# A prologue's second norm and its first two gated groups, taken batch by batch in 256-column matmuls and banks of their own

## The chip, the core and the metric

One core of a Trainium2 chip. The metric is the device time of one execution in microseconds. The program works on its eight pairs of sequences one after another, in one launch. The kernel before took 775.72 us (median of 3 runs, 775.19 to 776.27).

## What is computed

The input x has 16 sequences of 256 rows and 256 features, and so has the context. One layer of cross attention (an mLSTM form with 8 heads of 32), then a gated feed-forward net with hidden size 1024, both with a norm ahead of them and added to the residual. Cut to what matters:

```python
x = x + xattn(layernorm(x), ctx, ctx, ifgate_w, ifgate_b, outnorm_w)
z2 = layernorm(x)
h = silu(z2 @ w1.T * w1_s) * (z2 @ w2.T * w2_s)
h = gelu(h @ h1.T * h1_s)
h = gelu(h @ h2.T * h2_s)
x = x + h @ w3.T * w3_s
```

## The kernel before, in words

Two sequences (batches 0 and 1) make a pair: 512 rows in Q = 4 tiles of 128, tiles 0 and 1 of batch 0, tiles 2 and 3 of batch 1. The eight pairs run one behind the other. In the steady part the attention of pair i + 1 is woven into the feed-forward net of pair i; the attention of pair 0 stands alone in a prologue, and the change is at its end.

Each engine has its program written out by hand, and semaphores tie them. In the prologue's last part VectorE computes the second norm of pair 0 into `z2`, one tile at a time (`first_norm_apply`, L811), and TensorE transposes each tile into PSUM (`turn_first`, L1263): features on partitions, rows on the free axis. PSUM is two tensors of four banks, `ps_a` and `ps_f`, each bank 512 float32 wide. The features make two halves c of 128; half c of all 512 rows goes to bank c of `ps_a`. Then the transposed norm is split for exactness in two float32r parts: ScalarE copies it to the high part `z2_hi` (`take_z2T`, L668 and L670), VectorE subtracts that from the PSUM value to the low part `z2_lo` (L1053, L1055). In the trace these two are named after the buffers in which they lie, h_hi and h_lo.

The gated layer has KH = 8 groups m of 128 hidden units. A group needs two products, with w1 and with w2, each over two feature halves and two parts: eight matmuls of 512 columns into two banks of `ps_f`, banks 0 and 1 for even m, 2 and 3 for odd m. Group 0 of pair 0 is `first_swiglu` (L1444), which orders the eight by what is ready: high half 0, high half 1, low half 0, low half 1. The other groups are `swiglu` (L1434 for the high part, L1435 for the low part). ScalarE applies silu to the first product (L678), VectorE multiplies with the second (L1067) and signals `s_hf`; ScalarE and VectorE then make the high and low part of the result (L682, L1072). A group m of 2 or more waits for `s_hf` of group m - 2, since it writes the same banks:

```python
if m >= 2:
    pe.wait_ge(s_hf, KH * i + m - 1)
```

Behind the gated layer come two hidden layers of 8 groups with 16 matmuls each (`hidden`, L1468 and L1469) and the projection (L1503, L1504), which has matmuls of 256 columns.

`keep_clock` (L1587) issues matmuls of the identity that nobody reads; it stands twice near the change, with 24 before the transposes and with 2 behind them. `running_max` (L885) and `offsets` (L892 to L894) belong to pair 1's gates and stand on VectorE around the split. SP waits for the running maximum, stores it (`keep_rows`, L351) and spreads it over the partitions (`spread_max`, L362) for the masks of pair 1 (L917). `turn_rows` (L1336) transposes the gate rows behind group 2. ACT names ScalarE, DVE VectorE, PE TensorE and PEld its weight loads.

Of the kernel before, what the change touches and what calls it, by code (L numbers as in the profile page):

```python
# [7 lines left out]
ALU = mybir.AluOpType  # L8
ACT = mybir.ActivationFunctionType
AX = mybir.AxisListType  # L10
F32 = mybir.dt.float32
# [4 lines left out]
P = 128  # L16
BATCH, SEQ, DIM = 16, 256, 256
HEADS, DH = 8, 32
HID = 1024
TILES = SEQ // P  # L20
CH = DIM // P
KH = HID // P
# [10 lines left out]
W = 2  # L33
PAIRS = BATCH // W
NT = W * SEQ
Q = W * TILES
# [37 lines left out]
def build(nc, x, ctx_tok, ctx_t, gate_w, gate_b, outnorm_w, w_cols, scales, w3_s, out):  # L74
    with ExitStack() as stack:
        def sb(name, shape, dt=F32):
            return stack.enter_context(nc.sbuf_tensor(name, shape, dt))

        def sem(name):
            return stack.enter_context(nc.semaphore(name))  # L80
# [8 lines left out]
        z2_hi, z2_lo = h_hi[1][:, 0:CH], h_lo[1][:, 0:CH]  # L89
# [25 lines left out]
        z2 = num[:, 0:Q * DIM].rearrange("p (q d) -> p q d", q=Q)  # L115
# [7 lines left out]
        ident = sb("ident", [P, P])  # L123
# [16 lines left out]
        ps_f = stack.enter_context(nc.psum_tensor("ps_f", [P, 4, NT], F32))  # L140
        ps_a = stack.enter_context(nc.psum_tensor("ps_a", [P, 4, NT], F32))
# [25 lines left out]
        s_z2_first = sem("s_z2_first")  # L167
        s_z2T_first = sem("s_z2T_first")
        s_z2hi_first = sem("s_z2hi_first")
        s_z2lo_first = sem("s_z2lo_first")  # L170
# [51 lines left out]
        s_z2T = sem("s_z2T")  # L222
        s_z2hi = sem("s_z2hi")
        s_z2lo = sem("s_z2lo")

        s_ab = sem("s_ab")
# [16 lines left out]
        def first(j):  # L243
            return isinstance(j, int) and j == 0
# [29 lines left out]
        def score_out(j, b, rowgrp):  # L274

            return ps_f[:, rowgrp] if first(j) and b else ps_a[:, rowgrp]

        def value_out(j, b, t):

            if first(j):  # L280
                return (ps_f if b else ps_a)[:, 2 + t, 0:HEADS * DV]
            return ps_a[:, 2 + b, 0:HEADS * DV]
# [8 lines left out]
        def reuse(eng, semaphore, value):  # L291

            if not (isinstance(value, int) and value <= 0):
                eng.wait_ge(semaphore, value)
# [11 lines left out]
        def weights_in(eng, layer):  # L306
            eng.wait_ge(s_wgt[layer], 16 * sum(n == layer for n, _ in LOADS))
# [246 lines left out]
        def _(act):  # L554
# [109 lines left out]

            def take_z2T(j):
                if first(j):
                    act.wait_ge(s_z2T_first, 1)
                    act.activation(z2_hi[:, 0], ps_a[:, 0], ACT.Copy).then_inc(s_z2hi_first, 1)  # L668
                    act.wait_ge(s_z2T, 1)
                    act.activation(z2_hi[:, 1], ps_a[:, 1], ACT.Copy).then_inc(s_z2hi, 1)  # L670
                    return
                act.wait_ge(s_z2T, j + 1)
                act.activation(z2_hi, ps_a[:, 0:CH], ACT.Copy).then_inc(s_z2hi, 1)
# [96 lines left out]
        def _(dve):  # L770
# [96 lines left out]
            def shift_g(j):  # L867
                n = SCAN_STEPS * j
                f = f_row
                dve.wait_ge(s_scan, n + 1)  # L870

                g = rows[ROW_G:ROW_G + BH]
                dve.scalar_tensor_tensor(g, g, CAP, f, ALU.mult, ALU.add).then_inc(s_scan, 1)
                dve.wait_ge(s_scan, n + 2)
# [5 lines left out]
            def running_max(j):  # L880
                n = SCAN_STEPS * j
                f, m = f_row, m_row
                g = rows[ROW_G:ROW_G + BH]
                reuse(dve, s_mst, 16 * (j - 1))
                dve.tensor_tensor_scan(m, g, g, -MASKED, ALU.max, ALU.max).then_inc(s_scan, 1)  # L885
                dve.wait_ge(s_scan, n + 3)
# [162 lines left out]

            def take_z2T(j):  # L1050
                if first(j):
                    dve.wait_ge(s_z2hi_first, 1)
                    dve.tensor_tensor(z2_lo[:, 0], ps_a[:, 0], z2_hi[:, 0].bitcast(F32), ALU.subtract).then_inc(s_z2lo_first, 1)  # L1053
                    dve.wait_ge(s_z2hi, 1)
                    dve.tensor_tensor(z2_lo[:, 1], ps_a[:, 1], z2_hi[:, 1].bitcast(F32), ALU.subtract).then_inc(s_z2lo, 1)  # L1055
                    return
                dve.wait_ge(s_z2hi, j + 1)
                dve.tensor_tensor(z2_lo, ps_a[:, 0:CH], z2_hi.bitcast(F32), ALU.subtract).then_inc(s_z2lo, 1)
# [161 lines left out]
            scan_f(1)  # L1220
            first_norm_apply(2, xs[0], z2, s_z2_first)
            shift_g(1)
            running_max(1)
            take_z2T(0)
            offsets(1)
            dve.wait_ge(s_scl, 16)
            for i in range(PAIRS):
# [14 lines left out]
        def _(pe):  # L1242
# [15 lines left out]
            def turn_first(src, ready, half_done, done):  # L1258

                for q in range(Q):  # L1260
                    pe.wait_ge(ready, q + 1)
                    for c in range(CH):
                        last = pe.transpose(ps_a[:, c, q * P:(q + 1) * P], src[:, q, c * P:(c + 1) * P], ident[:])  # L1263
                        if q == Q - 1:
                            last.then_inc(done if c else half_done, 1)
# [145 lines left out]
            def columns(u, col, width, as_is):  # L1411

                if as_is:
                    slot = ORDER.index(u) % STAGE
                    return stage[:, slot * UNIT + col:slot * UNIT + col + width]
                return wgt[:, u * UNIT + col:u * UNIT + col + width]
# [4 lines left out]
            def swiglu(i, m, as_is):  # L1421
# [13 lines left out]
                        last = pe.matmul(ps_f[:, bank + half], w, moving(z2_lo[:, c], as_is), start=False, stop=(c == CH - 1))  # L1435
                last.then_inc(s_ab, 1)

            def first_swiglu():

                for part, landed in ((z2_hi, (s_z2hi_first, s_z2hi)), (z2_lo, (s_z2lo_first, s_z2lo))):  # L1440
                    for c in range(CH):
                        pe.wait_ge(landed[c], 1)
                        for half, base in enumerate((UNIT_W1, UNIT_W2)):
                            last = pe.matmul(ps_f[:, half], columns(base, c * P, P, False), part[:, c],  # L1444
                                             start=(part is z2_hi and c == 0), stop=(part is z2_lo and c == CH - 1))
                last.then_inc(s_ab, 1)

            def hidden(i, layer, m, ks, as_is):
                group = KH * layer + m
# [77 lines left out]
            def batch(i, a_stage, g_stage, as_is=False, last=False):  # L1527
                j, g = i + 1, i + 2
                if as_is:
                    pe.wait_ge(s_y, W * i)  # L1530
                weights_in(pe, 0)
                if not first(i):
                    pe.wait_ge(s_z2lo, i + 1)
                if first(i):
                    first_swiglu()
                for m in range(1 if first(i) else 0, KH):
                    swiglu(i, m, as_is)
                    if first(i) and m == 2:
                        turn_rows(1)
                    if a_stage and m == 4:  # L1540
                        scores(j, 0)

                def after_2(m):
                    if a_stage and m == 3:
                        scores(j, 1)
                    if a_stage and m == 5:
                        make_state(j)
                        values(j, 0, 0)
                        values(j, 0, 1)

                def after_3(m):
                    if g_stage and m == 2:
                        gates(g)
                    if a_stage and m == 7:
                        turn_z2(j)
                    if g_stage and m == 7:
                        turn_rows(g)

                def within_2(m):
                    if a_stage and m == 7:  # L1560
                        read_state(j)
                        values(j, 1, 0)
                        values(j, 1, 1)

                def between_2(k):
                    pass

                def between_3(k):
                    if g_stage and k == 3:
                        turn_z(g)  # L1570

                def within_3(m):
                    pass

                weights_in(pe, 1)
                hidden_layer(i, 0, as_is, between_2, within_2, after_2)
                weights_in(pe, 2)
                hidden_layer(i, 1, as_is, between_3, within_3, after_3)
                weights_in(pe, 3)
                project(i, as_is, last)  # L1580
                if last:
                    count_inexact()

            def keep_clock(products, bank=3):

                for _ in range(products):
                    pe.matmul(ps_f[:, bank, 0:P], ident[:], ident[:], start=True, stop=True)  # L1587
# [30 lines left out]
            plain_gates_normed(1)  # L1618
            keep_clock(24, 1)
            pe.wait_ge(s_zTe, 2)  # L1620
            turn_first(z2, s_z2_first, s_z2T_first, s_z2T)
            keep_clock(2, 1)
            for i in range(PAIRS):
                batch(i, i + 1 < PAIRS, i + 2 < PAIRS, last=i == PAIRS - 1)

# [54 lines left out]
```

## Time and profile before

| what | us |
|---|---|
| median of 3 runs | 775.72 (775.19 to 776.27) |
| the profiled execution | 775.79 |
| its span | 773.9 |
| TensorE busy | 764.5 (99%) |
| weight loads busy | 640.6 (83%) |
| VectorE busy | 545.8 (71%) |
| ScalarE busy | 381.6 (49%) |
| GpSimd busy | 50.9 (7%) |
| mean granted TensorE clock | 0.996 |

The span is what the profiler saw between the first and the last instruction; the time of the execution has 1.9 us more around it. An engine counts as busy while one of its instructions runs; matmuls are pipelined, and their ends are modelled, so that the step from one start to the next tells more than the duration. The granted clock is the share of full speed (2.4 GHz) that TensorE got.

### The profile page before, as it was taken

What the parts mean: (1) busy time and instruction counts of PE and PEld (TensorE: products, weight loads), DVE (VectorE), ACT (ScalarE), POOL (GpSimd) and SP (SyncE); (2) the same over time, 40 slices, a digit from 0 to 9 for tenths busy, and PEclk for the clock granted to TensorE, in tenths of its full rate; (3) what the DMA queues carried; (4) which work ended last, traced back from release to release, by engine and by line L of the source; (5) the groups of instructions that cost most, each with busy time, mean ns of one, the idle gap of its engine ahead of it and who ended that gap; (6) DMA issues with size and microseconds to landing.
All of it is one profiled execution on the core that took longest, in us unless ns stands there. A gap on an engine that the chain in (4) does not pass through costs nothing.

```text
span 773.9 us, 14930 instructions
## 1 busy us (share of the span) xinstructions
PE 764.5 (99%) x6170; PEld 640.6 (83%) x6170; DVE 545.8 (71%) x1294; ACT 381.6 (49%) x570; POOL 50.9 (7%) x63
## 2 busy tenths in 40 slices
PE   8999999999999999999999999999999999999997
PEld 7878888878888888878888888888889788888886
DVE  6787867586856969578675877758695684965544
ACT  3455645464554733556445564636435562445331
POOL 3300020000200011000200002000020000000000
PEclk9999999999999999999999999999999999999999
DMA  8933010501122000320005000130102100541540
GB/s 338 368 124 115 29 30 28 191 1 35 52 100 92 28 30 27 122 71 29 30 28 189 2 30 29 69 151 9 50 29 110 54 1 3 185 142 29 162 137 29
DMA packets 14615, 63.43 MB, mean 82 GB/s; under 512 B 2016, under 2 KB 2896, under 8 KB 11728
## 3 DMA queue, kind: packets, MB, share of 16 engines
q1 hardware_dynamic: 12960, 50.12, 18.7%
q0 software_dynamic: 1296, 11.53, 3.8%
q8 instruction: 49, 0.80, 0.4%
q10 hardware_dynamic: 288, 0.79, 0.3%
q14 instruction: 22, 0.18, 0.1%
HBM read 53.94 MB, written 8.50 MB: 81 GB/s over the span
## 4 chain that ended last, share of the span: by engine, by line
PE 85%; DVE 11%; ACT 2%; issue 1%; POOL 0%; POOLq 0%; DVEq 0%; ACTq 0%
PE ps_f L1468 24%; PE ps_f L1469 23%; DVE decay L917 8%; PE ps_f L1434 8%; PE ps_f L1435 7%; PE ps_f L1503 4%; PE ps_f L1504 4%; PE ps_a L1356 2%; PE ps_a L1379 2%; DVE decay L933 2%; PE ps_a L1246 2%; PE ps_f L1587 1%; PE ps_a L1282 1%; PE ps_f L1302 1%; PE ps_a L1407 1%
## 5 line engine op out<-in xcount | busy, mean ns | idle before, releaser
L1468 PE MATMUL ps_f<-h_hi,wgt 128*128 128x512 f32 x1024 | 401.7, 392 | 0.0
L1469 PE MATMUL ps_f<-h_lo,wgt 128*128 128x512 f32 x1024 | 398.8, 389 | 0.0
L1468 PEld LDWEIGHTS ps_f<-h_hi,wgt 128*128 128x128 f32 x1024 | 192.2, 188 | 41.6 <-issue 0.6
L1469 PEld LDWEIGHTS ps_f<-h_lo,wgt 128*128 128x128 f32 x1024 | 192.3, 188 | 38.8
L691 ACT ACTIVATE work<-ps_f,scl 128x512 f32<-128x512 f32 x128 | 87.5, 684 | 161.2 <-PE ps_f L1469 160.6
L1076 DVE TENSOR_TENSOR h_lo<-work,h_hi 128x512 fp32r<-128x512 f32 x128 | 86.5, 689 | 98.2 <-ACT h_hi L696 97.1
L1434 PE MATMUL ps_f<-h_hi,wgt 128*128 128x512 f32 x252 | 99.8, 396 | 0.0
L1435 PE MATMUL ps_f<-h_lo,wgt 128*128 128x512 f32 x252 | 98.7, 392 | 0.0
L678 ACT ACTIVATE work<-ps_f,scl 128x512 f32<-128x512 f32 x64 | 44.1, 689 | 98.2 <-PE ps_f L1435 96.3
L696 ACT ACTIVATE h_hi<-work 128x512 fp32r<-128x512 f32 x128 | 81.0, 633 | 4.1
L1067 DVE SCALAR_TENSOR_TENSOR work<-ps_f,scl,work 128x512 f32<-128x512 f32 x64 | 48.0, 750 | 47.0 <-ACT work L678 47.0
L917 DVE SCALAR_TENSOR_TENSOR decay<-decay,cols,future 128x128 f32<-128x128 f32 x224 | 64.5, 362 | 0.0
L1503 PE MATMUL ps_f<-wgt,h_hi 128*128 128x256 f32 x256 | 62.3, 285 | 0.0
L1504 PE MATMUL ps_f<-wgt,h_lo 128*128 128x256 f32 x256 | 61.7, 283 | 0.0
L1434 PEld LDWEIGHTS ps_f<-h_hi,wgt 128*128 128x128 f32 x252 | 47.3, 188 | 14.7 <-DVE work L1067 3.8
L1435 PEld LDWEIGHTS ps_f<-h_lo,wgt 128*128 128x128 f32 x252 | 47.4, 188 | 8.6
L1504 PEld LDWEIGHTS ps_f<-wgt,h_lo 128*128 128x128 f32 x256 | 49.1, 192 | 0.0
L1503 PEld LDWEIGHTS ps_f<-wgt,h_hi 128*128 128x128 f32 x256 | 49.0, 192 | 0.0
L621 ACT ACTIVATE decay<-decay 128x1024 f32<-128x1024 f32 x28 | 29.7, 1061 | 35.3 <-DVE decay L917 35.3
L1072 DVE TENSOR_TENSOR h_lo<-work,h_hi 128x512 fp32r<-128x512 f32 x64 | 43.7, 682 | 0.8
L682 ACT ACTIVATE h_hi<-work 128x512 fp32r<-128x512 f32 x64 | 39.9, 623 | 2.4 <-DVE work L1067 2.4
L933 DVE SCALAR_TENSOR_TENSOR decay<-ps_a,decay 128x512 f32<-128x512 f32 x60 | 37.1, 677 | 0.7 <-PE ps_a L1356 0.7
(195 smaller groups left out, 701.1 us busy)
## 6 DMA issues: line engine op xcount, KB each, us to landing
decay<-m_rows SPq DMA_DIRECT2D x14, 1024.0 KB, 6.1
decay<-w_cols SPq DMA_DIRECT2D x22, 512.0 KB, 4.2
wgt<-w_cols POOLq DMA_DIRECT2D x5, 1024.0 KB, 11.8
v_aug<-ctx_tok SPq DMA_DIRECT2D x8, 528.0 KB, 4.0
wgt<-w_cols POOLq DMA_DIRECT2D x2, 2048.0 KB, 14.4
x_kept<-xs SPq DMA_DIRECT2D x8, 512.0 KB, 2.6
xs<-x SPq DMA_DIRECT2D x7, 512.0 KB, 3.6
ctxT<-ctx_t SPq DMA_DIRECT2D x7, 512.0 KB, 3.3
```

The source lines that it names most:

```text
L691: act.activation(work[:, m % GELU], ps_f[:, (turn_of(i) + m) % 4], ACT.Gelu, scale=scl[:, 2 + layer, m:m + 1]).then_inc(s_gelu, 1)
L696: act.activation(h_hi[1 - layer][:, m], work[:, m % GELU], ACT.Copy).then_inc(s_hi, 1)
L917: last = dve.scalar_tensor_tensor(part, part, cols[:, t, row:row + 1], future[:], ALU.subtract, ALU.add)
L933: dve.scalar_tensor_tensor(s, score_out(j, b, r).rearrange("p (c n) -> p c n", c=CH), SCORE_SCALE, s, ALU.mult, ALU.mult)\
L1067: dve.scalar_tensor_tensor(work[:, 2 + m % 2], ps_f[:, bank], scl[:, 1, m:m + 1], work[:, m % 2], ALU.mult, ALU.mult).then_inc(s_hf, 1)
L1076: dve.tensor_tensor(h_lo[1 - layer][:, m], work[:, m % GELU], h_hi[1 - layer][:, m].bitcast(F32), ALU.subtract).then_inc(s_lo, 1)
L1434: pe.matmul(ps_f[:, bank + half], w, moving(z2_hi[:, c], as_is), start=(c == 0), stop=False)
L1435: last = pe.matmul(ps_f[:, bank + half], w, moving(z2_lo[:, c], as_is), start=False, stop=(c == CH - 1))
L1468: pe.matmul(ps_f[:, bank], w, moving(h_hi[layer][:, k], as_is), start=(k == 0), stop=False)
L1469: last = pe.matmul(ps_f[:, bank], w, moving(h_lo[layer][:, k], as_is), start=False, stop=(k == KH - 1))
L1503: pe.matmul(to, moving(h_hi[0][:, k, q * P:(q + 1) * P], as_is), w, start=(k == 0), stop=False)
L1504: last = pe.matmul(to, moving(h_lo[0][:, k, q * P:(q + 1) * P], as_is), w, start=False, stop=(k == KH - 1))
```

## The change

The transposed norm of batch b goes to banks 2b and 2b + 1 of `ps_a`, into the first 256 columns of each, one bank per feature half. ScalarE's copy and VectorE's subtraction take a batch at a time, both halves in one instruction of 128 x 2 x 256. `first_turn_z2` takes the place of `turn_first` for z2, and the two `keep_clock` products behind it are gone. `first_swiglu` now holds groups 0 and 1, in matmuls of 256 columns: for batch 0 the high parts of group 0 and group 1, then the low parts of both; for batch 1 high and low of group 0, then high and low of group 1. The list `steps` writes this order out. VectorE does its split before the running maximum of pair 1.

```diff
+        def first_z2T(b):
+            return ps_a[:, W * b:W * b + CH, 0:SEQ]
...
             def take_z2T(j):
                 if first(j):
-                    act.wait_ge(s_z2T_first, 1)
-                    act.activation(z2_hi[:, 0], ps_a[:, 0], ACT.Copy).then_inc(s_z2hi_first, 1)
-                    act.wait_ge(s_z2T, 1)
-                    act.activation(z2_hi[:, 1], ps_a[:, 1], ACT.Copy).then_inc(s_z2hi, 1)
+                    for b, (turned, done) in enumerate(((s_z2T_first, s_z2hi_first), (s_z2T, s_z2hi))):
+                        act.wait_ge(turned, 1)
+                        act.activation(z2_hi[:, :, b * SEQ:(b + 1) * SEQ], first_z2T(b), ACT.Copy).then_inc(done, 1)
                     return
...
                 if first(j):
-                    dve.wait_ge(s_z2hi_first, 1)
-                    dve.tensor_tensor(z2_lo[:, 0], ps_a[:, 0], z2_hi[:, 0].bitcast(F32), ALU.subtract).then_inc(s_z2lo_first, 1)
-                    dve.wait_ge(s_z2hi, 1)
-                    dve.tensor_tensor(z2_lo[:, 1], ps_a[:, 1], z2_hi[:, 1].bitcast(F32), ALU.subtract).then_inc(s_z2lo, 1)
+                    for b, (high, done) in enumerate(((s_z2hi_first, s_z2lo_first), (s_z2hi, s_z2lo))):
+                        at = slice(b * SEQ, (b + 1) * SEQ)
+                        dve.wait_ge(high, 1)
+                        dve.tensor_tensor(z2_lo[:, :, at], first_z2T(b), z2_hi[:, :, at].bitcast(F32), ALU.subtract).then_inc(done, 1)
                     return
...
             shift_g(1)
+            take_z2T(0)
             running_max(1)
-            take_z2T(0)
             offsets(1)
...
+            def first_turn_z2():
+
+                for q in range(Q):
+                    b, t = q // TILES, q % TILES
+                    pe.wait_ge(s_z2_first, q + 1)
+                    for c in range(CH):
+                        last = pe.transpose(first_z2T(b)[:, c, t * P:(t + 1) * P], z2[:, q, c * P:(c + 1) * P], ident[:])
+                    if t == TILES - 1:
+                        last.then_inc(s_z2T if b else s_z2T_first, 1)
+
             def first_swiglu():
 
-                for part, landed in ((z2_hi, (s_z2hi_first, s_z2hi)), (z2_lo, (s_z2lo_first, s_z2lo))):
+                high, low = (z2_hi, (s_z2hi_first, s_z2hi)), (z2_lo, (s_z2lo_first, s_z2lo))
+                steps = [(0, m, part) for part in (high, low) for m in range(2)] + [(1, m, part) for m in range(2) for part in (high, low)]
+                for b, m, (part, landed) in steps:
+                    at = slice(b * SEQ, (b + 1) * SEQ)
+                    pe.wait_ge(landed[b], 1)
                     for c in range(CH):
-                        pe.wait_ge(landed[c], 1)
                         for half, base in enumerate((UNIT_W1, UNIT_W2)):
-                            last = pe.matmul(ps_f[:, half], columns(base, c * P, P, False), part[:, c],
+                            last = pe.matmul(ps_f[:, 2 * m + half, at], columns(base, (m * CH + c) * P, P, False), part[:, c, at],
                                              start=(part is z2_hi and c == 0), stop=(part is z2_lo and c == CH - 1))
-                last.then_inc(s_ab, 1)
+                    if b == W - 1 and part is z2_lo:
+                        last.then_inc(s_ab, 1)
...
-                for m in range(1 if first(i) else 0, KH):
+                for m in range(2 if first(i) else 0, KH):
...
-            turn_first(z2, s_z2_first, s_z2T_first, s_z2T)
-            keep_clock(2, 1)
+            first_turn_z2()
```

TensorE's order at the end of the prologue, before the change: the transposes (of z2, which lies in num), the two clock products, group 0 (L1444), and the first rows of group 1.

```order
L1587 MATMUL ps_f<-ident 128x128 x24
L1263 MATMUL ps_a<-ident,num 128x128 x8
L1587 MATMUL ps_f<-ident 128x128 x2
L1444 MATMUL ps_f<-h_hi,wgt 128x512 x4
L1444 MATMUL ps_f<-h_lo,wgt 128x512 x4
L1434 MATMUL ps_f<-h_hi,wgt 128x512
L1435 MATMUL ps_f<-h_lo,wgt 128x512
```

The same place in the changed kernel, where L1459 is the matmul of the new `first_swiglu`; the last two rows are the first of group 2.

```order
L1603 MATMUL ps_f<-ident 128x128 x24
L1446 MATMUL ps_a<-ident,num 128x128 x8
L1459 MATMUL ps_f<-h_hi,wgt 128x256 x8
L1459 MATMUL ps_f<-h_lo,wgt 128x256 x8
L1459 MATMUL ps_f<-h_hi,wgt 128x256 x4
L1459 MATMUL ps_f<-h_lo,wgt 128x256 x4
L1459 MATMUL ps_f<-h_hi,wgt 128x256 x4
L1459 MATMUL ps_f<-h_lo,wgt 128x256 x4
L1436 MATMUL ps_f<-h_hi,wgt 128x512
L1437 MATMUL ps_f<-h_lo,wgt 128x512
```

Group 0 was the first eight matmuls of 512 columns. Now its share of the thirty-two is spread: four of the first eight, four of the second eight, and the next eight; the last of it is the 24th, and the last eight are group 1's.

VectorE's order at the same place, before: the last norm step, the shift, the running maximum, the two splits, the three rows of the offsets, the product of group 0.

```order
L811 TENSOR_SCALAR num<-xs,mv,nw 128x256 x4
L873 SCALAR_TENSOR_TENSOR rows<-rows,state 16x256
L885 SCALAR_TENSOR_TENSOR state<-rows 16x256
L1053 TENSOR_TENSOR h_lo<-ps_a,h_hi 128x512
L1055 TENSOR_TENSOR h_lo<-ps_a,h_hi 128x512
L892 TENSOR_TENSOR rows<-state 16x256
L893 TENSOR_SCALAR rows<-rows,state 16x128
L894 TENSOR_SCALAR rows<-state 16x128
L1067 SCALAR_TENSOR_TENSOR work<-ps_f,scl,work 128x512 x2
```

And in the changed kernel:

```order
L813 TENSOR_SCALAR num<-xs,mv,nw 128x256 x4
L875 SCALAR_TENSOR_TENSOR rows<-rows,state 16x256
L1057 TENSOR_TENSOR h_lo<-ps_a,h_hi 128x2x256 x2
L887 SCALAR_TENSOR_TENSOR state<-rows 16x256
L894 TENSOR_TENSOR rows<-state 16x256
L895 TENSOR_SCALAR rows<-rows,state 16x128
L896 TENSOR_SCALAR rows<-state 16x128
L1069 SCALAR_TENSOR_TENSOR work<-ps_f,scl,work 128x512 x2
```

The running maximum (L885, now L887) has gone behind the two splits; the rest keeps its order. SP's list of transfers is the same in both.

## Rows read from the trace of the kernel before

**Rows 1.** The page, part 1: busy time, share of the span, instructions.
```profile
PE 764.5 (99%) x6170; PEld 640.6 (83%) x6170; DVE 545.8 (71%) x1294; ACT 381.6 (49%) x570; POOL 50.9 (7%) x63
```

**Rows 2.** The page's chain by engine; who waited for whom (us, times, longest).
```profile
PE 85%; DVE 11%; ACT 2%; issue 1%; POOL 0%; POOLq 0%; DVEq 0%; ACTq 0%
...
PEld ps_f L1434 <- DVE work L1067: 3.8, 21, 0.3
```

**Rows 3.** Timeline, TensorE, 48 to 56 us: start, us, engine, instruction, [idle before <- releaser].
```profile
49.33 1.31 PE L1263 MATMUL ps_a<-ident,num 128*128 128x128 f32 x8
50.48 0.61 PE L1587 MATMUL ps_f<-ident 128*128 128x128 f32 x4
51.32 1.16 PE L1444 MATMUL ps_f<-h_hi,wgt 128*128 128x512 f32 x4 [0.22 <-ACT h_hi L668]
52.31 1.12 PE L1444 MATMUL ps_f<-h_lo,wgt 128*128 128x512 f32 x4
53.27 0.39 PE L1434 MATMUL ps_f<-h_hi,wgt 128*128 128x512 f32 x1
...
54.86 0.39 PE L1435 MATMUL ps_f<-h_lo,wgt 128*128 128x512 f32 x1
55.14 0.50 PE L1434 MATMUL ps_f<-h_hi,wgt 128*128 128x512 f32 x1
```

**Rows 4.** Timeline, TensorE, 49.6 to 49.75 us: the first four transposes.
```profile
49.33 0.67 PE L1263 MATMUL ps_a<-ident,num 128*128 128x128 f32 x4
```

**Rows 5.** Timeline, ScalarE, 50 to 57 us.
```profile
50.58 0.60 ACT L668 ACTIVATE h_hi<-ps_a 128x512 fp32r<-128x512 f32 x1 [1.12 <-PE ps_a L1263]
...
53.53 0.69 ACT L678 ACTIVATE work<-ps_f,scl 128x512 f32<-128x512 f32 x1 [1.87 <-PE ps_f L1444]
```

**Rows 6.** Timeline, VectorE, 50 to 57 us.
```profile
50.19 0.42 DVE L873 SCALAR_TENSOR_TENSOR rows<-rows,state 16x256 f32<-16x256 f32 x1
50.64 0.68 DVE L885 TENSOR_TENSOR_SCAN state<-rows 16x256 f32<-16x256 f32 x1
51.35 0.69 DVE L1053 TENSOR_TENSOR h_lo<-ps_a,h_hi 128x512 fp32r<-128x512 f32 x1
51.96 0.68 DVE L1055 TENSOR_TENSOR h_lo<-ps_a,h_hi 128x512 fp32r<-128x512 f32 x1
...
53.32 0.27 DVE L894 TENSOR_SCALAR rows<-state 16x128 f32<-16x128 f32 x1
54.33 0.75 DVE L1067 SCALAR_TENSOR_TENSOR work<-ps_f,scl,work 128x512 f32<-128x512 f32 x1 [0.74 <-ACT work L678]
```

**Rows 7.** Timeline, TensorE and its weight loads in a projection: matmuls of 256 columns.
```profile
135.89 0.28 PE L1504 MATMUL ps_f<-wgt,h_lo 128*128 128x256 f32 x1
136.01 0.28 PE L1503 MATMUL ps_f<-wgt,h_hi 128*128 128x256 f32 x1
...
135.89 0.19 PEld L1503 LDWEIGHTS ps_f<-wgt,h_hi 128*128 128x128 f32 x1
```

**Rows 8.** Groups by form, ScalarE, 0 to 140 us: count, busy us, mean ns.
```profile
L656 ACT ACTIVATE num<-ps_a 128x528 f32<-128x528 f32 x1 | 0.6, 612 | 0.2 <-PE ps_a L1379 0.2
```

**Rows 9.** Windows: us, busy of PE, PEld, DVE, ACT, POOL; PEclk, DMA share, GB/s.
```profile
34.00:37.40 3.40, 3.40 (x33) 3.40 (x33) 2.52 (x4) 0.00 (x0) 0.00 (x0) 1.00 1.03 424
37.40:40.80 3.40, 3.40 (x14) 2.39 (x14) 2.44 (x8) 2.37 (x5) 0.00 (x0) 0.51 0.86 345
...
48.00:55.00 7.00, 6.70 (x40) 5.17 (x38) 5.99 (x16) 3.21 (x5) 0.00 (x0) 1.00 0.20 55
```

**Rows 10.** Timeline, SP and VectorE; of the decay tile, transfers from issue to landing.
```profile
51.35 0.33 SPq L351 DMA_DIRECT2D m_rows<-state  x1
52.78 0.80 SPq L362 DMA_DIRECT2D decay<-m_rows  x2
...
70.70 9.21 DVE L917 SCALAR_TENSOR_TENSOR decay<-decay,cols,future 128x128 f32<-128x128 f32 x32
...
DMA to landing us min/median/max: 4.8/5.9/7.1
```

## Prediction

> **What bounds the kernel now.** I read the page first: TensorE is busy 99% of the 773.9 us span [rows 1], and the chain that ended last is 85% TensorE [rows 2]. So what sets the end is the stream of matmuls, and in the list of waits the entry that bears on the place of the change is small: the weight loads of the gated layer waited for VectorE's gating step 21 times, 3.8 us in all, 0.3 us at the most [rows 2]. A change at one place of the prologue can then move the end by what it moves the stream behind that place, and by nothing more. The profiled execution took 775.79 us; its span lacks 1.9 us of that, and it lies 0.07 us above the median of the three runs, 775.72. A measurement can tell some 0.2%, 1.55 us, from no change.
>
> The place is 48 to 56 us. There I read the timelines of TensorE, ScalarE and VectorE beside each other. The norm's four tiles are transposed from 49.33 to 50.64 [rows 3]; ScalarE begins to copy channel half 0 at 50.58 [rows 5], and the first gated matmul starts at 51.32, 0.14 us after that copy has ended at 51.18 [rows 3, 5]. Group 0 needs eight 512-column matmuls: four from 51.32, four from 52.31, the last ending at 53.43 [rows 3], and silu starts 0.10 us later, at 53.53 [rows 5]. Silu 0.69 us, VectorE's gating product from 54.33 to 55.08 [rows 6]: then banks 0 and 1 may be written again, and group 2, which writes them, starts at 55.14 [rows 3]. From silu's start to group 2's start it is 1.61 us. Meanwhile group 1 runs from 53.27, its eighth matmul starting at 54.86; 7 steps in 1.59 us make 0.227 us each, so it would leave TensorE free at 55.09 [rows 3]. This is what the reader is to see: in the kernel before, the work of group 1 just covers silu and product of group 0. Two chains, one on TensorE and one over ScalarE and VectorE, end within 0.05 us of each other, and everything of batch 0 and later queues behind group 2.
>
> **The change, term by term.**
> *First start.* Batch 0 of the norm is tiles 0 and 1. Their four transposes end at 50.00 [rows 4]. The copy can start about 0.08 us later (between silu's 0.10 and the smaller gap at the old copy), at 50.08. It reads 512 elements per partition as before, out of two banks now. A two-bank read of 528 elements took 612 ns, against 0.60 us for 512 out of one [rows 5, 8], so I charge nothing for the second bank. It ends at 50.68; plus 0.14 us, the first gated matmul starts at 50.82, **0.50 us earlier**. The two clock products (four matmul records from 50.48 [rows 3]) go; they lay in a wait, and cost or give nothing.
>
> *Splitting low.* VectorE is free at 50.61, after the shift [rows 6], and the running maximum no longer stands ahead. It takes batch 0's low part from 50.80 to 51.49 and batch 1's until about 52.12 (0.69 and 0.68 us, overlapping as in the rows [rows 6]). TensorE wants them after eight and after twenty matmuls, later than 51.7 and 53.1. No wait there; the waits inside the old group 0 are gone.
>
> *The matmuls.* Sixteen of 512 columns become thirty-two of 256. Matmuls of 256 columns in the same types start 0.12 us apart, with their weight loads of 0.19 us overlapping [rows 7]. So the two groups want 32 x 0.12 = 3.84 us, plus some 0.08 for the first after a pause, where sixteen wanted 16 x 0.227 = 3.63. The lower bound of the step is half of 0.227, 0.114; the upper one is the load's own 0.19, if loads did not overlap here. I take 0.12, the row of the same form. The pair of groups ends at about 54.74 instead of 55.09.
>
> *When group 0 is complete.* Here lies the term that decides. The new order interleaves the groups: of thirty-two matmuls, the last of group 0 is the 24th, since group 1's batch-0 products (eight) are run before it. It starts at 50.82 + 0.08 + 23 x 0.12 = 53.66 and ends 0.28 later, 53.94. Before, the eighth ended at 53.43. Silu then starts at 54.04, **0.51 us later** than 53.53. The chain behind it is unchanged, 1.61 us, and group 2 starts at 55.65 instead of 55.14. TensorE, done at 54.74, stands for 0.9 us where it stood for 0.05. The half microsecond won at the start is spent, and as much again is lost: the wait moves from in front of group 0 to in front of group 2.
>
> The Trainium skill (TensorE: Matmul & The Clock Gate, section Back-to-back issue gap) gives the step of matmuls in isolation as columns over 2.4 GHz and 2.5 ns, about 109 ns at 256 columns. By it the 24th matmul would come 0.25 us earlier and the loss be an estimated 0.26 us; the rows show 0.12 us, and the sum goes by them.
>
> *Behind group 2.* Group 1's last short matmul starts near 54.6, its silu at about 55.0, and 1.61 us after that, at 56.6, group 3 may start, while TensorE reaches it only after the eight matmuls of group 2, past 57.4: no new wait. All later groups shift with group 2, and so does VectorE's long row of masks, which starts after the last low part of the layer (70.70 [rows 10]).
>
> *What is moved on VectorE and SP.* The running maximum goes behind both splits: from 50.64 to about 52.13, 1.5 us later. The offsets end at about 53.8 instead of 53.59 [rows 6]; the transposes of the rows stand behind group 2 on TensorE and want them at 55.65 + 8 x 0.227 = 57.5; VectorE's product of group 0 comes at 54.8, so 1 us of cover remains. SP's store of the maxima was issued at 51.35 and its two broadcasts from 52.78 [rows 10]; the four transfers behind them on SP's queue (scale of w3, next values, kept x, next x) move by 1.5 us too; their readers come after the masks. The broadcasts landed at most 7.1 us after issue, by 60.2; with the shift 61.7, and their reader starts at 70.70 [rows 10]. Cost nothing, with 9 us of cover. If that went, a late landing would delay masks and scores.
>
> Sum: -0.50 us for the start. From the first gated matmul to the end of group 0 it was 53.43 - 51.32 = 2.11 us and becomes 0.08 + 23 x 0.12 + 0.28 = 3.12, so +1.01. Together +0.51; all other terms are hidden. On the profiled time 775.79 + 0.51 = 776.3, on the median **776.2 us**. Bounds: step 0.114 gives 23 x 0.006 = 0.14 less, 776.1; step 0.19 gives 23 x 0.07 = 1.6 more, 777.8.
>
> **Rivals.**
> *A: the early start is kept.* If group 2 were not held by silu and product of group 0, it would start at 54.74, 0.40 us earlier than before: 775.3. For it: TensorE bounds the whole, and the half microsecond of earlier start is real. Against: group 2's first load waits for the product already now, 55.14 against 55.08 [rows 3, 6], and for A silu must start by 53.13, only 2.3 us after the first matmul, while the 24th ends 3.1 us after the first has started.
> *B: swallowed.* The shift disappears in a later wait (masks, scores), 775.7. The masks hang on the same stream, so both sides of that wait shift: little for it.
> *C: slower, by the clock.* TensorE fell from its upper to its lower level, 2.4 to 1.2 GHz, in the prologue: the granted clock is 0.51 from 37.4 to 40.8 us, after 3.4 us of matmuls, nearly all of 33 columns, that count as fully busy [rows 9]. The new hole of 0.9 us, without the two clock products, might bring such a stretch: 3.4 us at half clock cost 1.7 us of matmul time, with the 0.5 together 2.2 us, 777.9. It decides if the granted clock falls between 54 and 60 us. Against: from 48 to 55 us the clock is at 1.00 although TensorE idles 0.3 of 7 us [rows 9], and dense 512-column work follows the hole at once. The Trainium skill (same page, section A second HAM failure mode: psum-queue depth-cycling) says that short pauses between groups of matmuls can make the clock swing between its levels. No row of the kernel before shows such a swing, its waits between groups being far shorter than 0.9 us.
> *D: loads bound the short matmuls,* the 0.19 us step: 777.8. Against: [rows 7], the same form at 0.12.
> *E: not what it says.* The order shows the 32 short matmuls and both splits in their new places; no chance is set aside for this.
>
> **How the numbers follow.** Forecast (group 2 held, +0.3 to +0.7) 0.75; A 0.09; B 0.06; C 0.07; D 0.03. The predicted time is the forecast's, 776.2. The range takes in A's 775.3 and, above, half a microsecond of spread of the runs and a step between 0.12 and 0.19: 775.2 to 777.3. It leaves out C and D. Faster by over 0.2% would need 774.2, which no case gives: 0.02. Slower by over 0.2% needs 777.3: C and most of D, 0.08. The rest, 0.90, is within.
>
> **What would show it.** In the new timeline of TensorE: first 256-column gated matmul near 50.8, starts 0.12 apart, the 32nd near 54.6, a gap of some 0.9 us, group 2 near 55.65 released by VectorE's product; silu 0 near 54.0; clock 1.00 throughout 48 to 56. Wrong if group 2 starts before 55.2, if the step is above 0.14, if the granted clock falls there, or if the first layer's later groups do not carry the shift.

## The result, and the profile after

The changed kernel takes 778.95 us (median of 7 runs, 778.62 to 780.92). Beside it on the same chips the kernel before took 776.15 us (7 runs, 775.19 to 776.99). The ratio is 1.0041, 95% interval 1.0032 to 1.0050: slower by 0.4%, some 2.8 us. I had forecast no difference that can be told, with 776.2 us and a range up to 777.3. The profiled execution took 780.78 us, with a span of 778.9. One execution of all those below, in the second series of the reordered kernel, took 1022.28 us at a mean granted clock of 0.695, and no ratio has it in.

At the place of the change nearly everything came as worked out. TensorE's timeline there, in the columns of [rows 3]:

```profile
49.32 1.32 PE L1446 MATMUL ps_a<-ident,num 128*128 128x128 f32 x8
50.77 1.19 PE L1459 MATMUL ps_f<-h_hi,wgt 128*128 128x256 f32 x8
51.79 1.12 PE L1459 MATMUL ps_f<-h_lo,wgt 128*128 128x256 f32 x8
52.75 0.64 PE L1459 MATMUL ps_f<-h_hi,wgt 128*128 128x256 f32 x4
53.23 0.64 PE L1459 MATMUL ps_f<-h_lo,wgt 128*128 128x256 f32 x4
...
54.19 0.64 PE L1459 MATMUL ps_f<-h_lo,wgt 128*128 128x256 f32 x4
55.58 0.50 PE L1436 MATMUL ps_f<-h_hi,wgt 128*128 128x512 f32 x1 [0.75 <-DVE work L1069]
```

The first gated matmul is at 50.77 (51.32 in [rows 3]), four short matmuls take 0.48 us from start to start (0.12 each), group 0's last ends at 53.87, and group 2 begins at 55.58 instead of 55.14, after 0.75 us in which TensorE waits for VectorE's product. ScalarE and VectorE, to be read against [rows 5, 6]:

```profile
50.02 1.25 ACT L672 ACTIVATE h_hi<-ps_a 128x512 fp32r<-128x512 f32 x2 [0.59 <-PE ps_a L1446]
53.97 0.69 ACT L680 ACTIVATE work<-ps_f,scl 128x512 f32<-128x512 f32 x1 [2.70 <-PE ps_f L1459]
```

```profile
50.72 1.29 DVE L1057 TENSOR_TENSOR h_lo<-ps_a,h_hi 128x512 fp32r<-128x512 f32 x2
51.93 0.67 DVE L887 TENSOR_TENSOR_SCAN state<-rows 16x256 f32<-16x256 f32 x1
...
53.28 0.27 DVE L896 TENSOR_SCALAR rows<-state 16x128 f32<-16x128 f32 x1
54.77 1.56 DVE L1069 SCALAR_TENSOR_TENSOR work<-ps_f,scl,work 128x512 f32<-128x512 f32 x2 [1.22 <-ACT work L680]
```

So the local shift is +0.44 us. That leaves some 2.4 us of the 2.8 unexplained, and they are not in the prologue. Among the waits of the changed kernel (who waited for what: us in total, times, longest) three rows of TensorE and its weight loads bear on this. The first is the local wait and has its counterpart in [rows 2]; the last two have none before:

```profile
PEld ps_f L1436 <- DVE work L1069: 4.1, 19, 1.0
...
PEld ps_a L1381 <- issue: 2.6, 1, 2.6
PE ps_a L1381 <- issue: 2.5, 1, 2.5
```

"issue" is time in which the engine waited for nothing that the profile shows. It happens once, 586 us behind the place of the change, in the attention stage of the last pair. TensorE's timeline there:

```profile
639.38 0.46 PE L1373 MATMUL ps_a<-v_aug,num 128*32 128x33 f32 x32
639.66 1.31 PE L1381 MATMUL ps_a<-v_aug,decay 128*32 128x33 f32 x125
643.48 0.25 PE L1381 MATMUL ps_a<-v_aug,decay 128*32 128x33 f32 x3 [2.52 <-issue]
```

The kernel before runs the same stretch in one piece, a state product of 32 tiny matmuls (L1371) and 128 value matmuls (L1379):

```profile
638.66 0.46 PE L1371 MATMUL ps_a<-v_aug,num 128*32 128x33 f32 x32
638.94 1.34 PE L1379 MATMUL ps_a<-v_aug,decay 128*32 128x33 f32 x128
640.21 0.50 PE L1468 MATMUL ps_f<-h_hi,wgt 128*128 128x512 f32 x1
```

A hole of 2.5 us, three matmuls before the stretch's end, for which the profile names no semaphore, no operand and no other engine. What the reader can count: 32 + 125 = 157 matmuls, each with its weight load, are 314 instructions in 1.6 us (two in about 10 ns), then nothing, then the last 6 of 320. The windows of the changed kernel around it (columns as in [rows 9]) show TensorE idle in the hole, and no transfer that starts in it (a transfer counts where it starts; one does so just before):

```profile
640.00:641.00 1.00, 0.97 (x110) 0.85 (x97) 0.13 (x1) 0.81 (x2) 0.00 (x0) 1.00 0.09 16
...
641.00:643.50 2.50, 0.02 (x2) 0.02 (x2) 1.18 (x2) 0.00 (x0) 0.00 (x0) 1.00 0.00 0
643.50:644.70 1.20, 1.20 (x8) 1.00 (x9) 0.00 (x0) 0.61 (x1) 0.00 (x0) 1.00 0.05 14
644.70:648.20 3.50, 3.50 (x10) 2.78 (x9) 0.00 (x0) 0.00 (x0) 0.00 (x0) 0.53 0.00 0
```

The last row is a second effect: TensorE's granted clock falls from 2.4 to 1.2 GHz for some 3.4 us, a little over 1 us behind the hole. That costs half of it, 1.7 us, and the span of this execution is 5.0 us above that of before: 0.44 + 2.5 + 1.7 = 4.6, and 0.4 more. Of these, 0.3 had built up before the hole: the stretch starts at 639.38 instead of 638.66, 0.72 us late; why the 0.44 grew to 0.72 is open. Five of the seven runs are at 778.6 to 779.1 and two at 780.8 to 780.9; the two groups lie about 2 us apart, near the price of such a stretch of half clock. The profiled execution, 780.78, is one of the two, and the other, 780.92, has the lowest mean granted clock of the seven, 0.992.

### The profile page after: what moved, and what is told of

Its sections match the earlier page's. It is cut to its first block, busy times and chain, and to the rows that moved or that the text cites. A ratio compares the mean times of both kernels' runs of the same rounds, so it can differ in the third digit from the quotient of the medians.

```text
span 778.9 us, 14954 instructions
## 1 busy us (share of the span) xinstructions
PE 766.4 (98%) x6182; PEld 642.7 (83%) x6182; DVE 546.0 (70%) x1294; ACT 381.7 (49%) x570; POOL 51.1 (7%) x63
## 4 chain that ended last, share of the span: by engine, by line
PE 85%; DVE 11%; ACT 2%; issue 2%; POOL 0%; POOLq 0%; DVEq 0%; ACTq 0%
PE ps_f L1484 24%; PE ps_f L1485 23%; DVE decay L919 8%; PE ps_f L1436 8%; PE ps_f L1437 7%; PE ps_f L1519 4%; PE ps_f L1520 4%; PE ps_a L1381 2%; PE ps_a L1358 2%; DVE decay L935 2%; PE ps_a L1248 2%; PE ps_f L1603 1%; PE ps_a L1284 1%; PE ps_f L1304 1%; PE ps_a L1409 1%
```

## What could make a hole 586 us behind the change

**Theory F, code.** The trace has a DMA queue of kind "instruction". On the page of the kernel before:

```profile
q8 instruction: 49, 0.80, 0.4%
```

49 transfers and 0.80 MB are 16 KB each. TensorE's 12,340 matmul and load records (6170 each, [rows 1]) over 49 are about 252: one transfer for some 250 of its instructions. The Trainium skill (Runtime: NRT & Kernel Launch, section Instruction fetch mechanics) says that instruction memory is refilled in blocks of 16 KiB, 256 instructions, the next one being fetched while the current one is executed, and calls the cost of crossing a boundary "mostly hidden". The count agrees with the first; the hole would be a case of the second where it is not hidden. At the 5 ns an instruction of this stretch, a block is used up in 1.3 us. If a boundary lies early in the stretch, and the next one, 256 on, still in it, the block behind it may come too late. The change adds 24 instructions to TensorE, 12 matmul records and their loads, as the page after shows:

```profile
PE 766.4 (98%) x6182; PEld 642.7 (83%) x6182; DVE 546.0 (70%) x1294; ACT 381.7 (49%) x570; POOL 51.1 (7%) x63
```

So each boundary falls 24 earlier in the program's later parts. In the changed kernel a block would end at instruction 314 of the stretch, in the kernel before at 338, 18 behind it. And a block was on its way: of the two us from 639 to 641, the DMA view of the changed kernel has one packet of the instruction queue.

```profile
q8 instruction: 1, 0.02, 4.5%
```

4.5% of 16 engines over 2 us are 1.4 us; by the window above it started between 640 and 641, and from 636 to 646 us the view has but two packets, both of this queue. That speaks against contention with other transfers. If the block before began at instruction 314 - 256 = 58 of the stretch, the array was there at about 639.7, and it went on at 643.48: an estimated 3.8 us for a block, against 1.3 us in which the stretch uses one up. From the start of the packet, 640.6, it is 2.9 us. From one attention stage to the next there are 1569 of TensorE's instructions (1556 matmul and load records, 13 separate waits), which is 6 x 256 + 33, so that the boundary wanders 33 earlier per stage; that is why a kernel's seven stages differ. Each stage has a second stretch, of 128 value matmuls alone (at 646.79 us in the kernel before); no profile here has a hole in one.

**Theory L, local.** The rival: something that the change itself does (the banks, the split, the transfers moved by 1.3 us, the wait of group 2) surfaces late as a wait that the profile does not name.

## The experiments

**Padding the kernel before.** No part of the change, only instructions:

```diff
+            for _ in range(48):
+                pe.wait_ge(s_ident, 1)
             pe.wait_ge(s_ident, 5)
             keep_clock(14)
```

> The kernel before, with 48 waits that are long satisfied put at the head of TensorE's program, which the build makes into 24 instructions; everything else is untouched. Theory F (fetch of TensorE's code): the 2.5 us hole in the values of the last attention stage comes from where a block of 256 instructions ends, and the change moved that place by the 24 instructions it adds. Then this kernel has the hole of the changed kernel without the change: no instruction of TensorE for 2.3 to 2.7 us in the values near 641 us (minus the 0.4 us of the local shift), 314 matmul and load records into that stretch, and a time of 778.2 to 778.8 us. Theory L (the change's own waits, transfers or order cause it): no hole, and the time is that of before within 0.3 us.

Measured: the hole is there, after the same 32 + 125 matmuls. TensorE's timeline:

```profile
640.98 0.46 PE L1371 MATMUL ps_a<-v_aug,num 128*32 128x33 f32 x32
641.26 1.30 PE L1379 MATMUL ps_a<-v_aug,decay 128*32 128x33 f32 x125
645.01 0.25 PE L1379 MATMUL ps_a<-v_aug,decay 128*32 128x33 f32 x3 [2.45 <-issue]
```

The time is 779.86 us (4 runs, 779.3 to 782.3) beside 776.34, ratio 1.0044 (1.0028 to 1.0059). It is 1 us more than I expected. The first clock product starts at 3.73 instead of 2.13 us, and the gated layer at 52.26 instead of 51.32; 2.45 for the hole and 0.94 for this would be 3.4 of the 3.5 us. That the waits cause the 0.94 is not shown: in front of the transposes TensorE waits 1.7 us for VectorE here, and in the kernel with 6 instructions added (below), whose first clock product is 0.09 us late, the gated layer still starts 0.73 us late, at 52.05. In this profile 3.4 us of half clock also lie in the gated layer, from 51.2 us, where the kernel before had them from 37.4 [rows 9]. Theory L falls: a kernel without any of the change has the hole.

**The changed kernel with 24 instructions fewer.**

```diff
-            keep_clock(18)
+            keep_clock_wide(6)
+            keep_clock(6)
```

where the new helper multiplies with the identity read twice, 256 columns in one matmul, so that six take the array time of twelve.

> The changed kernel, with 12 of the 18 clock products ahead of the maxima's spread written as 6 of twice the columns: the same TensorE time, 24 matmul and load instructions fewer. Theory F: block ends lie where they lay in the kernel before, so the hole near 641 us is gone, and the time is that of before plus the local shift of 0.44 us: 776.4 to 776.9. Theory L: the hole and the 2.8 us stay, 778.7 to 779.2.

Measured: 776.60 us (11 runs, 775.85 to 777.73), ratio to the kernel before 1.0005 (0.9996 to 1.0014). There is no hole; in its list of waits no entry of the value matmuls (L1381) remains, and the local wait is unchanged:

```profile
PE ps_f L1436 <- DVE work L1069: 0.8, 1, 0.8
```

Its gated layer is that of the changed kernel to 0.02 us (group 2 at 55.59). So with the boundaries back in place the whole change costs 0.45 us by the timeline and 0.3 us by the medians, which the interval does not tell from nothing, and the loss of 2.8 us is gone.

**Another amount, another stage.**

> The kernel before with 57 such instructions ahead (114 waits). From one attention stage to the next the block ends come 33 instructions earlier in the stretch of values. Theory F: with 57 instructions the last stage's block end leaves the range where it hurts, and the stage before it takes the place: the hole of about 2.5 us is near 549 us, 91 us earlier than in the changed kernel, and none is near 641; the time is again 778 to 779. Theory L, or a hole that belongs to the last stage for another reason (data, transfers): none near 549.

Measured, TensorE's timeline of that kernel:

```profile
552.80 0.46 PE L1371 MATMUL ps_a<-v_aug,num 128*32 128x33 f32 x32
553.07 1.30 PE L1379 MATMUL ps_a<-v_aug,decay 128*32 128x33 f32 x125
556.89 0.25 PE L1379 MATMUL ps_a<-v_aug,decay 128*32 128x33 f32 x3 [2.51 <-issue]
```

The hole has moved to the stage before, at the same instruction 314, and the last stage has none:

```profile
648.43 0.46 PE L1371 MATMUL ps_a<-v_aug,num 128*32 128x33 f32 x32
648.71 1.34 PE L1379 MATMUL ps_a<-v_aug,decay 128*32 128x33 f32 x128
```

By the step of 33 a block ends there at instruction 281, with 256 tiny instructions in it, and costs nothing; nor does the end at 256 in the first stage of the changed kernel (314 + 6 x 33 = 512 = 2 x 256). So a block of tiny instructions does not make a hole by itself. The packets of the instruction queue differ: that of the last stage here starts at 646.5 us, 1.9 us ahead of the stretch, that of the changed kernel's hole at 640.6, 1.2 us behind the start of its stretch. What lets a packet start, the runs do not show.

Back to the hole of this kernel. It comes at 554.4 us instead of 549, since 114 waits hold the start back: the first clock product is at 7.28 us, 5.2 us late. That start, the hole and one more stretch of half clock behind it (window below), 5.2 + 2.5 + 1.7 = 9.4 us, make up the 785.75 us of its single run.

```profile
558.10:561.50 3.40, 3.40 (x10) 2.60 (x9) 0.30 (x1) 0.00 (x0) 0.00 (x0) 0.52 0.00 0
```

**How far the boundary must move.** Three smaller paddings, 24, 12 and 36 waits (12, 6 and 18 instructions).

> The kernel before with 24 satisfied waits (12 instructions) at the head. The block end in the last stage's values comes to 326, six instructions behind the stretch of 320, where it was 338 in the kernel before (no hole) and 314 in the changed one (2.5 us). Theory F with a stream that TensorE's sequencer works off ahead of the array: the six slow instructions (0.11 us each) are cover, so a hole of 1.5 to 2.1 us, now behind the values, in front of a hidden layer's matmuls near 641 us. If the hole were all or nothing by whether the end lies in the stretch: none. Theory L: none.

> The same with 12 waits (6 instructions): block end at 332, twelve slow instructions of cover. Theory F: a hole of 0.8 to 1.5 us near 641 us, behind the values; between b_pad12 and the kernel before (338, none seen). All or nothing: none.

> The kernel before with 36 satisfied waits (18 instructions): block end at 320, just at the end of the values, with no slow instruction as cover. The holes so far: 2.5 us at 314, 1.33 at 326, 0.39 at 332, none at 338. Theory F: 2.1 to 2.5 us, directly behind the last value matmul near 641 us. A hole of another size, or within the values, speaks against the count.

The lines at the hole, of the kernels with 18, with 12 and with 6 instructions:

```profile
640.75 1.34 PE L1379 MATMUL ps_a<-v_aug,decay 128*32 128x33 f32 x128
644.32 0.50 PE L1468 MATMUL ps_f<-h_hi,wgt 128*128 128x512 f32 x1 [2.23 <-issue]
```

```profile
641.17 0.50 PE L1468 MATMUL ps_f<-h_hi,wgt 128*128 128x512 f32 x1
641.51 0.39 PE L1469 MATMUL ps_f<-h_lo,wgt 128*128 128x512 f32 x1
641.74 0.40 PE L1468 MATMUL ps_f<-h_hi,wgt 128*128 128x512 f32 x1
643.47 0.50 PE L1469 MATMUL ps_f<-h_lo,wgt 128*128 128x512 f32 x1 [1.33 <-issue]
```

```profile
642.21 0.40 PE L1469 MATMUL ps_f<-h_lo,wgt 128*128 128x512 f32 x1
642.99 0.51 PE L1468 MATMUL ps_f<-h_hi,wgt 128*128 128x512 f32 x1 [0.39 <-issue]
```

With 18 the hole is right behind the 160 matmuls (320 instructions); with 12 it is three hidden matmuls further (326), with 6 six matmuls further (332, the first at 640.94): each at the counted instruction.

| block ends at instruction | kernel | hole, us |
|---|---|---|
| 281 | 57 added (last stage) | none |
| 314 | changed kernel; 24 added; 57 added (stage before) | 2.52; 2.45; 2.51 |
| 320 | 18 added | 2.23 |
| 326 | 12 added | 1.33 |
| 332 | 6 added | 0.39 |
| 338 | kernel before; 24 taken from the changed kernel | none |

The place was foretold to the instruction; the size at 320 lies in my range, those at 326 and 332 below theirs (1.5 to 2.1 and 0.8 to 1.5). I had charged 0.11 us of cover for an instruction; six of them shortened the hole by 0.9 us, 0.15 each. The switch from tiny to wide matmuls, which has steps of 0.34 us and not 0.23 (641.17 to 641.51), accounts for part of it. The kernel before stands 6 instructions from a block end with a hole. The single executions of the three took 781.44, 778.39 and 777.35 us; these do not follow the holes alone, since the profiles differ in the prologue as well: its stretch of half clock, 3.4 us in the kernel before, lasts 6.8 us in the first two and is missing in the third.

**Making the stretch shorter instead.** In the changed kernel, with its 24 instructions, the values are cut in two:

```diff
                         make_state(j)
                         values(j, 0, 0)
+                    if a_stage and m == 6:
                         values(j, 0, 1)
```

and ScalarE's `take_near` goes from m = 5 to m = 6.

> The changed kernel, without the 24 instructions taken out, but with the 256 records of values cut in two: the values of batch 1 come behind hidden group 6 instead of group 5 (and ScalarE's copy of them behind its gelu 6). No stretch of tiny matmuls is then as long as a block of 256, so by theory F no place of the block ends can cost a hole in it: no hole in any values, and 776.3 to 777.0, as a_thin24. Theory L, or fetching that is slow at that place whatever the instructions are: a hole near 641 us remains, 778.5 or more. If the later copy delays the gelus, TensorE shows waits of up to 1 us in front of group 7 in each stage, up to 7 us.

Measured: 778.80 us (6 runs, 777.92 to 779.3), ratio 1.0033 (1.0021 to 1.0045). No hole, as foretold, yet nothing gained. Its waits say why:

```profile
PEld ps_a L1373 <- issue: 2.5, 7, 0.4
PEld ps_a L1381 <- issue: 2.5, 7, 0.4
```

The second row is new: entering tiny matmuls from wide ones leaves the weight loads idle for 0.36 us, and now each of the seven stages does it once more. The time puts it at (778.80 - 776.38 - 0.44) / 7 = 0.28 us a stage, 2 us in all; the profile has more, (640.69 - 90.72) / 6 = 91.66 us from one stretch's start to the next where the changed kernel has 91.30, 0.36 a stage. No row has TensorE wait for the gelus, so the later copy is not the cause. The cure costs nearly as much as the one hole that it prevents.

**The order of the short matmuls.** With the 24 instructions taken out, all of group 0 first:

```diff
-                steps = [(0, m, part) for part in (high, low) for m in range(2)] + [(1, m, part) for m in range(2) for part in (high, low)]
+                steps = [(b, m, part) for m in range(2) for b in range(2) for part in (high, low)]
```

> As a_thin24, and the order of the 32 short matmuls is all of group 0 (batch 0, batch 1), then all of group 1. By my reading of group 2's wait (silu and product of group 0 hold it), group 0 is complete near 53.0 instead of 53.9, and group 2 starts near 54.7, about 0.4 us before the start it had in the kernel before (55.14): 775.5 to 776.1 under theory F. If group 2's start does not hang on group 0's last matmul, it stays at 55.6 and the time at that of a_thin24. Under theory L some 2.5 us come on top of either.

Measured: 775.80 us (11 runs, 775.0 to 776.43), ratio 0.9994 (0.9985 to 1.0003); and once more:

> a_m0first once more in five rounds, to tell its 775.8 from the 776.3 of the kernel before: theory F and the wait of group 2 on group 0's product give 775.5 to 776.1 again, a ratio below 1 by 0.0003 to 0.0009; if the first measurement was luck, a ratio of 1.000 or above.

776.02 us (median of 11 runs) beside 776.07, ratio 0.9996 (0.9987 to 1.0006). TensorE's timeline in the second:

```profile
50.84 0.71 PE L1459 MATMUL ps_f<-h_hi,wgt 128*128 128x256 f32 x4
51.55 0.74 PE L1459 MATMUL ps_f<-h_lo,wgt 128*128 128x256 f32 x4
...
54.52 0.64 PE L1459 MATMUL ps_f<-h_lo,wgt 128*128 128x256 f32 x4
54.99 0.45 PE L1436 MATMUL ps_f<-h_hi,wgt 128*128 128x512 f32 x1
```

Group 2 starts at 54.99, 0.6 us before the changed kernel's and 0.15 before the start in [rows 3], and right behind the last short matmul, with no wait (I had expected 54.7). In the profile of the first series the whole prologue is 0.45 us later and group 2 starts at 55.45. From the first transpose to group 2 the two profiles agree, 5.61 and 5.60 us, beside 5.81 in the kernel before and 6.26 in the changed one: group 2's start did hang on when group 0 is complete. The gain of the batch-wise split survives only in this order, at 0.2 us of the 0.5 by which the first matmul is early. Against the kernel before neither series tells a difference; against the changed kernel this version is some 3.5 us faster, by the ratios.

With the cut of the values as well:

> a_split with the 32 short matmuls in the order of a_m0first (all of group 0, then all of group 1). Expected as a_m0first, 775.5 to 776.2, without any number of instructions being tuned; the version to keep if it holds.

778.47 us (11 runs, 777.2 to 778.96), ratio 1.0026 (1.0017 to 1.0035): wrong by the switches, as a_split.

## Why the prediction was wrong, point by point

- *First start*: worked out 50.82, measured 50.77. The two-bank copy cost nothing extra (each 0.60 us, as in [rows 5]). Right.
- *Splitting low*: from 50.72 and done by 52.01, never waited for. Right.
- *The matmuls*: step 0.12 us, the row of the same form held. The 109 ns that follow, as an estimate, from the formula of the Trainium skill for isolated matmuls (TensorE: Matmul & The Clock Gate, section Back-to-back issue gap) did not.
- *When group 0 is complete*: silu at 53.97 (worked out 54.04), group 2 at 55.58 (55.65), shift +0.44 (+0.51). The term I called decisive was right in mechanism, sign and size. The kernel with 24 instructions fewer has it alone, in its timeline (group 2 at 55.59); its time, 776.60, lies within the noise of before.
- *Running maximum and SP*: the offsets ended at 53.55, hidden as said.
- *Rival C* (the clock falls behind the 0.8 us wait in the prologue): no. It fell elsewhere, behind a hole three times as long. The windows of the prologue after:

```profile
48.00:55.00 7.00, 6.57 (x51) 5.70 (x49) 5.43 (x16) 3.44 (x6) 0.00 (x0) 1.00 0.01 2
55.00:60.00 5.00, 4.42 (x21) 3.63 (x21) 3.22 (x5) 2.65 (x5) 0.00 (x0) 1.00 0.89 375
```

- *Rivals A, B, D*: none. B did not come: the last stage's stretch is still 0.72 us late. A's early group 2 needs another order.
- **The step that failed** is the sentence in the sum, "all other terms are hidden", and the one behind it, that the later groups merely shift with group 2. I priced sixteen more matmuls by their time on the array and never as instructions. With the four clock records gone TensorE's stream is 24 longer (12 matmul records and their loads), and this moved every later block boundary by 24 against the seven stretches of 320 tiny matmuls and loads; one boundary came from 18 instructions behind such a stretch to 6 inside its end. Price 2.5 us, and in some runs 1.7 us of half clock on top. No cost on my list had its place behind the prologue, and so the range ended at 777.3.

Could it have been foreseen? The instruction queue stands on the page before, and the step of 33 per stage can be counted from the order. The latency of a block does not stand in the trace of before, where no stage ran dry; with it unknown, a hole somewhere behind would have been a rival, and the range would have had to reach higher; the 2.5 us are known only from these runs.

## What to carry to other kernels

In a long unrolled program on an engine that is busy all the time, the number of instructions is a term of its own: count what an edit adds to the stream ahead of every dense stretch (here 5 ns for an instruction, 256 of them in 1.3 us; such a stretch is where a hole can come, not where it must), and if a change far from a hole moves it, pad or thin the program by a few instructions before believing any local story. And when a layer's first groups are interleaved, the moment that counts is when the first group is complete, not when the first matmul starts; a wait that moves from in front of one group to in front of another has saved nothing.

## What the runs showed of the hardware beyond that

- A block boundary is cheap nearly everywhere: about 49 in the program, and 0 or 1 holes. It hurts where the next block arrives after the array has used up the last one. By the table it costs 2.5 us with the boundary 6 instructions inside the stretch's end, and nothing when 18 instructions of wide matmuls (0.11 us each, the first ones slower) lie before the boundary; with the end at 281 or 256, behind 256 tiny instructions, it cost nothing; the packet had started ahead of the stretch (646.5 against 648.43 us, and 89.7 against 91.56).
- In the profiles with a hole of 2.2 us or more (the changed kernel, and the kernels with 18, 24 and 57 instructions added) TensorE's granted clock fell to half within 2 us behind it, for about 3.4 us; behind those of 1.33 and 0.39 us it did not. It does not seem to happen each time: of the changed kernel's seven runs two are 2 us slower. One of them is the profiled one, with the fall; that the other had it is likely by its size and its granted clock of 0.992, not shown, and that the five had none likewise.
- Satisfied waits at the head of TensorE's program are not free: with 12, 24 and 57 of these instructions it starts at 2.41, 3.73 and 7.28 us, which is 0.11 us each. With 6 it starts at 2.22 beside 2.13; there it waits for GpSimd's identity anyway.
- A kernel's prologue differs from profile to profile by a stretch of half clock: none in those of the kernel with 6 instructions added and of the one with its values cut, 6.8 us with 12 and with 18 added, 3.4 us in the others. Its price there is not one number: without it the gated layer starts at 49.92 us with the values cut and at 50.77 with it in the changed kernel, yet at 52.05 without it with 6 instructions added and at 51.32 with it in the kernel before.
- Every entry from wide into tiny matmuls costs 0.36 us of idle weight loads, and 0.3 to 0.4 us of time.
